# Routing stage of a fused graph and expert kernel: the order of two TensorE products, and where the second slot table is made

## The reference, cut to what matters

```python
def _L1_gnn_ref(x, adj, weight, bias):           # third layer
    d_inv_sqrt = (jnp.sum(adj, axis=-1) + 1e-05) ** (-0.5)
    adj_norm = d_inv_sqrt[..., :, None] * adj * d_inv_sqrt[..., None, :]
    support = jnp.einsum('bni,io->bno', x, weight)
    return jnp.einsum('bnm,bmo->bno', adj_norm, support) + bias

def _L1_ffn_ref(x, router_w, w1, w2, w3):        # fourth layer
    flat = x.reshape(-1, C)
    probs = jax.nn.softmax(flat @ router_w.T, axis=-1)
    topk_probs, topk_idx = jax.lax.top_k(probs, 2)
    topk_probs = topk_probs / (jnp.sum(topk_probs, axis=-1, keepdims=True) + 1e-09)
    gates = jnp.einsum('nk,nke->ne', topk_probs, jax.nn.one_hot(topk_idx, 8))
    h = jax.nn.silu(jnp.einsum('nc,ehc->neh', flat, w1)) * jnp.einsum('nc,ehc->neh', flat, w3)
    return jnp.einsum('ne,nec->nc', gates, jnp.einsum('neh,ech->nec', h, w2)).reshape(B, T, C)

x = x + _L1_gnn_ref(_layernorm(x), adj, ...)
x = x + _L1_ffn_ref(_layernorm(x), ...)
```

## Time and profile before

| | us |
|---|---|
| median of 3 runs | 1099.04 (1098.57 to 1100.66) |
| profiled execution, its own time | 1100.47 |
| its span, first to last instruction | 1098.7 |
| PE busy | 973.8 (89%) |
| DVE busy | 784.4 (71%) |
| ACT busy | 685.6 (62%) |
| POOL busy | 518.1 (47%) |

### The profile page before, as it was taken

The page is one execution under the profiler, slowest core; times in us unless marked ns, Lnnn a source line. Parts: engine busy times, 40 slices in busy tenths (PEclk is TensorE's granted clock), DMA queues, the critical chain, the costliest instruction groups (busy, mean ns, idle before and its releaser), DMA issues. The chain is left out here.

```text
span 1098.7 us, 23216 instructions
## 1 busy us (share of the span) xinstructions
PE 973.8 (89%) x6744; PEld 855.6 (78%) x6744; DVE 784.4 (71%) x2028; ACT 685.6 (62%) x1467; POOL 518.1 (47%) x512
## 2 busy tenths in 40 slices
PE   4999999999999578999999958863399999799997
PEld 3988998898899335766766847763299999799997
DVE  5788888888887568999999836998455555355553
ACT  4566656656665479888898638882255555355553
POOL 5233223322422017877778544577344444244454
PEclk9999999999999698999999969985599999899999
DMA  5221131122110032343233039634244443233331
GB/s 179 72 73 50 48 95 48 48 64 79 48 38 0 25 82 77 78 77 78 77 78 67 12 98 289 207 128 143 86 139 146 122 127 106 86 94 99 96 98 48
DMA packets 82408, 99.09 MB, mean 90 GB/s; under 512 B 9243, under 2 KB 68258, under 8 KB 82186
## 3 DMA queue, kind: packets, MB, share of 16 engines
q1 hardware_dynamic: 72122, 74.24, 24.9%
q0 software_dynamic: 8752, 21.25, 5.5%
q10 hardware_dynamic: 1440, 2.43, 0.6%
HBM read 72.26 MB, written 27.02 MB: 90 GB/s over the span
## 5 line engine op out<-in xcount | busy, mean ns | idle before, releaser
L1805 PE MATMUL e_p_y<-w,e_gT 128*128 (+1 forms) x852 | 118.3, 275 | 0.0
L1752 DVE TENSOR_TENSOR e_g<-e_sl,e_p_h 128x342 f32<-128x342 f32 x142 | 72.6, 511 | 63.9 <-ACT e_sl L1730 55.5
L1716 POOL DMA_INDIRECT sorted_scratch<-e_xg x71 | 69.0, 972 | 90.7 <-DVE e_xg L1762 87.7
L1714 POOL DMA_INDIRECT out<-e_xg x71 | 68.9, 970 | 87.1 <-DVE e_xg L1762 79.6
L1734 ACT ACTIVATE e_gT<-e_p_gx 128x384 f32<-128x384 f32 x142 | 69.6, 490 | 64.0 <-PE e_p_gx L1795 64.0
L1730 ACT ACTIVATE e_sl<-e_p_h 128x342 f32<-128x342 f32 x142 | 64.9, 457 | 69.7 <-PE e_p_h L89 69.7
L1805 PEld LDWEIGHTS e_p_y<-w,e_gT 128*128 128x128 f32 (+1 forms) x852 | 106.1, 192 | 0.4 <-issue 0.4
L87 PE MATMUL e_p_h<-w_hi,e_xT_hi 128*128 x284 | 104.7, 368 | 1.5 <-DVE e_g L1752 0.8
L1756 DVE TENSOR_TENSOR e_xT_lo<-e_p_gx,e_xT_hi 128x128 fp32r<-128x128 f32 x142 | 41.4, 292 | 86.4 <-ACT e_xT_hi L1738 86.0
L1009 DVE SCALAR_TENSOR_TENSOR m_c<-m_p_x,m_vecs,m_c 128x506 f32<-128x506 f32 (+2 forms) x144 | 95.5, 734 | 2.0 <-ACT m_c L873 1.8
L89 PE MATMUL e_p_h<-w_hi,e_xT_lo 128*128 x284 | 92.6, 326 | 0.0
(11 more groups left out here) (386 smaller groups left out, 3316.5 us busy)
## 6 DMA issues: line engine op xcount, KB each, us to landing
e_xg<-sorted_scratch SPq DMA_DIRECT2D x142, 130.0 KB, 2.1
m_cum<-cum_scratch SPq DMA_DIRECT2D x16, 1024.0 KB, 7.9
g_adjT<-in_adjT SPq DMA_DIRECT2D x16, 512.0 KB, 3.8
g_adj<-in_adj SPq DMA_DIRECT2D x16, 512.0 KB, 4.8
c_adjT<-in_adjT SPq DMA_DIRECT2D x16, 512.0 KB, 5.5
x_tokens<-in_x SPq DMA_DIRECT2D x16, 256.0 KB, 4.8
sorted_scratch<-nothing SPq DMA_DIRECT2D x2, 1040.0 KB
sorted_scratch<-nothing SPq DMA_DIRECT2D x12, 130.0 KB
```

The costliest lines, as they stand in the source:

```text
L1714: sent = pool.indirect_dma_start(out_dram, home, xg[:, b, RES:RES + P], None, bounds_check=NT * P - 1, oob_is_err=False)
L1716: sent = pool.indirect_dma_start(sorted_dram[1], home, xg[:, b], None, bounds_check=ROWS - 1, oob_is_err=False)
L1752: dve.tensor_tensor(g[:, i % D3], sl[:, i % 2], p_h3[i % 2][:, 0:HP], ALU.mult).then_inc(q["g_ready"], 1)
L1805: last = pe.matmul(p_y[d % 2][:, 0:P], gT[0:r, d % D3, k], w2k[:, bass.ts(e, P)], start=k == 0, stop=k == len(CH) - 1)
```

## The change

Two edits. In PE's turn of the routing stage, agg(i-1) now stands ahead of out(i-2); both keep their waits. And the second pass's slot table is no longer made in DVE's tail: a class `Slots` holds the table's buffers beyond the stage and makes it in four pieces. The first pass's four pieces stay in the tail; those of the second are made by DVE in the expert stage, at ticks 12, 16, 20 and 24, each ahead of that tick's other work. SP waits for the finished table before the first load of the second pass, and PE before the first word of it. The instructions of the table are the same, and each still waits for the one before it.

```diff
+class Slots:
+    PIECES = 4
+    def piece(self, dve, k, n, source, words, then):
+        if n == 0:
+            then(dve.tensor_tensor(past[:], slot_no[:]..., per_expert(self.ends[:, k]), ALU.is_ge))
+            then(dve.tensor_reduce(exp_f[:], past[:], AX.X, ALU.add))
+        elif n == 1:
+            then(dve.tensor_tensor(part[:], past[:], per_expert(self.tiles[:, k]), ALU.mult))
+            then(dve.tensor_reduce(first[:], part[:], AX.X, ALU.add))
+        elif n == 2:
+            then(dve.tensor_tensor(first[:], slot_no[:], first[:], ALU.subtract))
+            then(dve.scalar_tensor_tensor(out=first[:], in0=exp_f[:], scalar=float(PASS), in1=first[:], op0=ALU.mult, op1=ALU.add))
+            then(dve.tensor_scalar(source[:, k], first[:], float(P), None, ALU.mult))
+            then(dve.tensor_scalar(exp_f[:], exp_f[:], float(EX - 1), None, ALU.min))
+        else:
+            for j in reversed(range(QUAD - 1)):
+                then(dve.scalar_tensor_tensor(out=quad[:, :, j], in0=quad[:, :, j + 1], scalar=float(EX), in1=quad[:, :, j], ...))
+            then(dve.tensor_copy(words[:, k], quad[:, :, 0]))
...
@@ dispatch_phase, DVE's tail
-            for k in range(TOPK):
...
+            for piece in range(Slots.PIECES):
+                slots.piece(dve, 0, piece, source, words, then)
@@ dispatch_phase, PE
             for i in range(END):
                 o, a, e, f = i - OUT, i - AGG, i - TURN2, i - LOG
+                if live(a):
+                    need(pe, q["aggT_ready"], a - 1)
+                    pe.wait_ge(adjT_in[a % ADJ], 16 * (a // ADJ + 1))
+                    pe.wait_ge(q["xs_ready"], T * (a + 1))
...
                 if live(o):
 ...
-                if live(a):
...
@@ expert_phase
+    TABLE_TICKS = range(XG, XG + 4 * Slots.PIECES, 4)
@@ SP
                 if u == 0 and k:
                     sp.wait_ge(q["padded"], 16 * EX)
+                    sp.wait_ge(q["second_table"], 1)
@@ DVE
             for i in range(-TURN, TICKS + DOWN):
+                if i in TABLE_TICKS:
+                    slots.piece(dve, 1, TABLE_TICKS.index(i), source, words, then)
+                    if i == TABLE_TICKS[-1]:
+                        dve.sem_inc(q["second_table"], 1)
@@ PE, expert_of
+                if u == 0 and k:
+                    pe.wait_ge(q["second_table"], 1)
```

More of the change, by code:

```diff
@@ L1266, with __init__, sb, per_expert @@
 HOME, GATE = (P, P + 2), (P + 1, P + 3)
+class Slots:
+    PIECES = 4
+    def __init__(self, nc, ctx):
+        def sb(name, shape):
+            return ctx.enter_context(nc.sbuf_tensor("slots_" + name, shape, F32))
+        self.slot_no, self.tiles, self.ends = sb("no", [P, PASS]), sb("tiles", [P, TOPK, EX]), sb("ends", [P, TOPK, EX])
+        self.past, self.part = sb("past", [P, PASS, EX]), sb("part", [P, PASS, EX])
+        self.exp_f, self.first = sb("exp_f", [P, PASS]), sb("first", [P, PASS])
+    def piece(self, dve, k, n, source, words, then):
+        past, part, exp_f, first, slot_no = self.past, self.part, self.exp_f, self.first, self.slot_no
+        by_slot = [P, PASS, EX]
+        def per_expert(v):
+            return v.rearrange("p (a e) -> p a e", a=1).broadcast_to(by_slot)
+        if n == 0:
+            then(dve.tensor_tensor(past[:], slot_no[:].rearrange("p (s a) -> p s a", a=1).broadcast_to(by_slot), per_expert(self.ends[:, k]), ALU.is_ge))
+            then(dve.tensor_reduce(exp_f[:], past[:], AX.X, ALU.add))
[8 more added lines that the diff above has]
+        else:
+            quad = exp_f[:].rearrange("p (u j) -> p u j", j=QUAD)
+            for j in reversed(range(QUAD - 1)):
+                then(dve.scalar_tensor_tensor(out=quad[:, :, j], in0=quad[:, :, j + 1], scalar=float(EX), in1=quad[:, :, j], op0=ALU.mult, op1=ALU.add))
+            then(dve.tensor_copy(words[:, k], quad[:, :, 0]))
 def expert_weights(nc, ctx):
@@ L1275, in expert_weights, with dispatch_phase @@
     return pair("w1", [P, EX, HP]), pair("w3", [P, EX, HP]), w2
-def dispatch_phase(nc, w, X, norm, dinv, rows, source, words, filled, pad_at, nothing, experts, adjT_dram, sorted_dram, eye):
+def dispatch_phase(nc, w, X, norm, dinv, rows, source, words, filled, pad_at, nothing, slots, experts, adjT_dram, sorted_dram, eye):
     ADJ = 5
@@ L1298, in dispatch_phase @@
         before, ones = sb("before", [P, P]), sb("ones", [P, P])
-        slot_no = sb("slot_no", [P, PASS])
         bases = sb("bases", [P, KE])
@@ L1322, in dispatch_phase @@
         dest_f = sb("dest_f", [P, TOPK, TG])
-        count, tiles, ends = sb("count", [P, TOPK, EX]), sb("tiles", [P, TOPK, EX]), sb("ends", [P, TOPK, EX])
+        count = sb("count", [P, TOPK, EX])
         tiles_i = sb("tiles_i", [P, TOPK, EX], I32)
-        past, part = sb("past", [P, PASS, EX]), sb("part", [P, PASS, EX])
-        exp_f, first = sb("exp_f", [P, PASS]), sb("first", [P, PASS])
+        slot_no, tiles, ends = slots.slot_no, slots.tiles, slots.ends
         p_agg = [ph.psum(f"p_agg{p}", [P, S]) for p in range(2)]
@@ L1573, in _ @@
             then(dve.tensor_copy(filled[:], ends[:, 0, EX - 1:EX]))
-            by_slot = [P, PASS, EX]
-            def per_expert(v):
-                return v.rearrange("p (a e) -> p a e", a=1).broadcast_to(by_slot)
-            for k in range(TOPK):
[L1579 to L1590, removed]
+            for piece in range(Slots.PIECES):
+                slots.piece(dve, 0, piece, source, words, then)
             for n, (_, dst) in enumerate(weights):
@@ L1599, in _ @@
                 o, a, e, f = i - OUT, i - AGG, i - TURN2, i - LOG
+                if live(a):
+                    need(pe, q["aggT_ready"], a - 1)
+                    pe.wait_ge(adjT_in[a % ADJ], 16 * (a // ADJ + 1))
+                    pe.wait_ge(q["xs_ready"], T * (a + 1))
+                    for g in range(G):
+                        for h in range(2):
+                            last = pe.matmul(p_agg[a % 2][:, g * N:(g + 1) * N], xs[:, a % 2, 2 * g + h], adjT[:, a % ADJ, g, h], start=h == 0, stop=h == 1)
+                    last.then_inc(q["agg_done"], 1)
                 if live(o):
@@ L1633, in _, with expert_phase @@
                     last.then_inc(q["log_done"], 1)
-def expert_phase(nc, source, words, filled, pad_at, nothing, experts, sorted_dram, out_dram, eye):
+def expert_phase(nc, source, words, filled, pad_at, nothing, slots, experts, sorted_dram, out_dram, eye):
     XG, D3 = 12, 3
@@ L1657, in expert_phase @@
         p_y = [ph.psum(f"p_y{k}", [P, S]) for k in range(2)]
-        names = "p_g_clear turned x_hi x_split h1_done h3_done sl_ready g_ready gT_ready y_done y_ready padded"
+        names = "p_g_clear turned x_hi x_split h1_done h3_done sl_ready g_ready gT_ready y_done y_ready padded chain second_table"
         q = {s: sem(s) for s in names.split()}
@@ L1744, in _, with then @@
                 dve.memset(p_gx[k][:], 0.0).then_inc(q["p_g_clear"], 1)
+            count_ = [0]
+            def then(ins):
+                count_[0] += 1
+                ins.then_inc(q["chain"], 1)
+                dve.wait_ge(q["chain"], count_[0])
             for i in range(-TURN, TICKS + DOWN):
                 a, d = i + TURN, i - DOWN
+                if i in TABLE_TICKS:
+                    slots.piece(dve, 1, TABLE_TICKS.index(i), source, words, then)
+                    if i == TABLE_TICKS[-1]:
+                        dve.sem_inc(q["second_table"], 1)
                 if live(i):
@@ L1829, in build @@
         experts = expert_weights(nc, ctx)
+        slots = Slots(nc, ctx)
         sorted_dram = (scratch["sorted0"], scratch["sorted1"])
-        dispatch_phase(nc, ins, X, norm, inv[:, 0], rows, source, words, filled, pad_at, nothing, experts, ins["adjT"], sorted_dram, eye)
-        expert_phase(nc, source, words, filled, pad_at, nothing, experts, sorted_dram, out_dram.rearrange("b n d -> (b n) d"), eye)
+        dispatch_phase(nc, ins, X, norm, inv[:, 0], rows, source, words, filled, pad_at, nothing, slots, experts, ins["adjT"], sorted_dram, eye)
+        expert_phase(nc, source, words, filled, pad_at, nothing, slots, experts, sorted_dram, out_dram.rearrange("b n d -> (b n) d"), eye)
 def kernel(x, adj, L0_gnn_w_se, L0_gnn_b_se, L0_gnn_conv1_w, L0_gnn_bn1_g, L0_gnn_bn1_b, L0_gnn_bn1_m, L0_gnn_bn1_v,
```

## The result

The changed kernel takes 1103.28 us (median of 16 runs, 1100.39 to 1105.41), the kernel before 1100.83 in the runs beside it (16 runs, 1098.37 to 1102.88): ratio 1.002, 95% interval 1.0011 to 1.003, that is 1.2 to 3.3 us slower. The profiled execution took 1104.44 (span 1102.6).

The account below looks back on a forecast made before the run. Routing was bounded by time to the first scatter, VectorE's loop to group 4, then 32 scatters. 0 + 0 - 1.0 + 0.3 = -0.7 gave 1099.8 us for a profiled-like execution, 1098.3 for the median; range 1096.4 to 1101.2.

Parts of the forecast that it names:

- The table, 0 + 0: Second pass's slot table: 0 for the routing stage's end (-0.3 to +1.2), 0 for pieces in the expert stage.
- rule on two-input instructions: Expert stage: each long table piece could stand behind a scatter up to 0.97 us; some +0.6 in sum, kept at 0.
- The start, -1.0: Routing stage's start: agg(1) directly follows agg(0), out(0) comes behind; -1.0 us taken, between -2.0 and +0.1.
- my two cases: Routing stage's start: TensorE's clock rises as before at 659.1, +0.1 us; or as soon as agg(0) is over, -2.0.
- The loop, +0.3: Routing loop, 682 to 736: out behind agg, free at full clock, late in half-clock stretches; 0 to +2.2 us, +0.3 taken.
- rival 3: Routing loop: out behind agg holds VectorE's update, up to 2.2 us per half-clock step; two steps give 1102.4; chance 0.09.
- the 0.65 that I worked out: Routing loop at full clock: out, behind agg, is done 0.65 us before VectorE's update needs it; effect 0.

Follow-up runs that it names:

- the idle products: Whole change plus eight idle 128x128 TensorE products, ahead of its wait for normalised rows, in every turn that ranks a group; ratio 0.9996 to the kernel before.

## Why the prediction was wrong

**The table, 0 + 0: right.** With the table alone the stage behind its first scatter is as long as before (87.93 and 87.89), its two long scatters moved four places, and the pieces (12 instructions, not the 15 that I counted) cost about 0.17. The gating product came 1.07 late, about as worked out (830.93 - 829.71 = 1.22), and TensorE took nearly nothing from it. The Trainium skill's rule on two-input instructions that I weighed at +0.6 was not put to the test: the two-input instruction of each long piece ran at 0.75, but between two scatters and beside none (816.18 to 816.93; the scatters run from 815.01 to 815.98 and from 817.06 on).

**The start, -1.0: right.** -1.12 and -1.00 in the two profiles of the change. The clock rose some 10.7 us after the stage's start in place of 13.1, between my two cases. That the middle of the two came so near is luck in part: the same order at the start gave a first scatter at 45.02 to 46.05 in nine profiles, the old one 46.73 to 47.12 in three.

**The loop, +0.3: this is the term that failed.** It measured +2.08 and +1.83 in the two profiles of the change, and +4.73 with the order alone. The mechanism was on the list: rival 3 named the place, the half-clock stretches, and two steps as the point from which it decides; it gave 1102.4, measured were 1103.28, which lies near by luck in part (its 4.4 for the two steps was double what the loop lost, and the level, below, rose). What was wrong is the weight of 0.09. I read "such a stretch hits a step with the small cover only some of the time" off a trace with one such stretch. Of the three profiles with agg first throughout and no idle products in the loop, each has two whole agg at half clock (3.59 to 3.76), all in turns 9, 11, 13 or 15, and all six end in a wait. Of the kernels with out first in those turns (before, and seven of the experiments without idle products in the loop), each has one or two slow agg as well (2.51 to 3.62), and none ends in a wait. So the stretch was no mishap: all eleven of these profiles have it, and it was free because out stood ahead of it. Of the loop's +2.08 and +1.83 the update's waits are 1.6; in the first profile one VectorE instruction of 0.46 in place of 0.17 (737.27, beside a scatter) adds 0.3, and about 0.2 is not accounted for.

**Price.** I gave "up to 2.2" for a step with agg and out both slow, about 1 with a rise inside. Measured: 0.76 to 0.84 where out was back at full clock or nearly (1.05 to 1.17), 2.35 and 2.46 where it was slow too (1.91 and 1.48). The cover at full clock was larger than the 0.65 that I worked out: 0.94 and 0.91 in the changed kernel (turns 11 and 13), 0.98 and 0.90 with the idle products. In the trace each product group starts some 0.15 ahead of the end of the one before it, which I counted at the start and not here.

**The break.** I counted the work that moves, and not the idle time. Before, TensorE's idle time in a pair of turns was split, as two more rows of its timeline show:

```profile
682.08 1.13 PE L1606 MATMUL c_p_out<-c_weight,c_aggT 128*128 128x128 f32 x8 [0.46 <-ACT c_aggT L1463]
...
686.43 0.66 PE L1620 MATMUL c_p_xT<-eye,rows 128*128 128x128 f32 x4 [1.49 <-ACT c_xT L1443]
```

With agg first nothing is waited for at out, and 1.97 stands ahead of xT in one piece. In all three profiles the first such break (1.97 or 1.98) is followed by a half-clock agg in the next turn. But the length of a break doesn't decide it: in the changed kernel a longer one, 2.20, is followed by an agg at full clock, and a shorter one, 1.62, by one at half clock.

```profile
710.99 0.66 PE L1640 MATMUL c_p_xT<-eye,rows 128*128 128x128 f32 x4 [2.20 <-ACT c_xT L1478]
...
712.82 1.97 PE L1626 MATMUL c_p_agg<-c_adjT,c_xs 128*128 128x256 f32 x8
...
721.71 0.66 PE L1640 MATMUL c_p_xT<-eye,rows 128*128 128x128 f32 x4 [1.62 <-ACT c_xT L1478]
...
723.79 3.66 PE L1626 MATMUL c_p_agg<-c_adjT,c_xs 128*128 128x256 f32 x8
```

And the version with agg first in the first turns alone, where the break is 1.48, has a slow agg in the same turn as the change. Filling the breaks keeps the clock up; that joining them lets it fall is not shown.

**The level.** The median of before rose from 1099.04 (3 runs) to 1100.83 (16 runs). Of the 5.0 us between forecast and result, 1.8 are that; the other 3.2 are the change, +2.45 in place of -0.7.

**Open.** Why the clock falls in one of the four turns and not in another stays open. From the stage's first instruction to the end of the span the two profiles of the change are longer by 1.5 (454.26 and 454.22 in place of 452.73), within the timed 1.2 to 3.3; start, loop and pieces make about 1.1 of it. The profile of the order alone, where out was slow too, is longer by 3.4; how often that happens was not counted. The Trainium skill, TensorE: Matmul & The Clock Gate, Part 1, calls the number of slow products ahead of the clock's rise, at a kernel's start, run-variable; the loop's +1.83, +2.08 and +4.73 for one and the same order show such a spread in the middle of a kernel.

## What to carry to other kernels

Before an operation that somebody waits for is put behind a longer one, work out its cover with the longer one at half clock, and ask of several profiles how often that happens, not of one. An order that leaves the sum of the work alone still decides what stands behind a stretch of half clock. In a stage that a chain of transfers ends, shorten what holds the transfers first: cutting two long instructions in eight each took 3.2 us off the stage, where the whole change was forecast to gain 0.7.

## What was not expected of the hardware

- Two scatters that began within VectorE's subtractions of 128x2728 took 2.60 and 2.61, and one that began 0.03 us behind the start of the first (769.50) took 0.97; beside the same work in pieces of 128x341 (about 0.4 us each) they took 0.97 and 0.98, 3.2 us less in all. The Trainium skill, SBUF — State Buffer, section "Who interferes with whom", has it that the order of issue and not the operation's shape decides who waits; for two of the three that agrees, and the instruction's length decided how long they waited.
- Idle products on TensorE, 1.95 us in every second turn, took away the loss of a kernel whose clock falls: group 4 at 43.91 in place of 45.99.
